# Four graph layers on one core: the steps between the probabilities and the value products of layers 1 and 3, in another order

## The reference, cut to what matters

```python
h = jnp.maximum(_layernorm(x), 0.0); x = x + _L0_gnn_ref(h, adj, adj, ...)   # attention, 8 heads of 32
h = jnp.maximum(_layernorm(x), 0.0); x = x + _L1_gnn_ref(h, adj, ...)        # attention, 4 heads of 64
h = jnp.maximum(_layernorm(x), 0.0); x = x + _L2_gnn_ref(h, adj, ...)        # gated tanh graph layer
h = jnp.maximum(_layernorm(x), 0.0); x = x + _L3_gnn_ref(h, adj, ...)        # attention, 4 heads of 64
```

```python
sim = jnp.einsum('bhid,bhjd->bhij', q, k) * scale
sim = jnp.where(adjacency_mask[:, None, :, :], sim, neg)
attn = jax.nn.softmax(sim, axis=-1)
out = jnp.einsum('bhij,bhjd->bhid', attn, v)   # the value products
return out.transpose(...).reshape(...) @ Wo + bo   # the output projection
```

## Time and profile before

| what | value |
|---|---|
| median of 3 runs | 2009.05 us (2006.77 to 2009.29) |
| profiled execution | 2007.06 us, its span 2005.1 us |
| mean granted clock of PE | 0.967 |
| PE busy | 1840.9 us, 92% |
| DVE busy | 1380.0 us, 69% |
| ACT busy | 996.7 us, 50% |
| POOL busy | 153.3 us, 8% |

### The profile page before, as it was taken

One profiled execution on the slowest core, in us unless ns is written; L12 is line 12 of the kernel. 1 busy time (PEld: TensorE's weight loads), 2 busy tenths in 40 slices (PEclk: granted clock), 3 DMA queues, 4 the chain that ended last, 5 costly groups with the idle time before them and its releaser, 6 DMA issues.

```text
span 2005.1 us, 58180 instructions
## 1 busy us (share of the span) xinstructions
PE 1840.9 (92%) x23611; PEld 1636.5 (82%) x23611; DVE 1380.0 (69%) x3777; ACT 996.7 (50%) x3707; POOL 153.3 (8%) x265
## 2 busy tenths in 40 slices
PE   6999999899999999999999999999998999999997
PEld 5878888878888878888878887878887888888886
DVE  4576677676777676777676677676767676677674
ACT  4455455454455454455455455455455445455452
POOL 0000000000000000000000000000000000000000
PEclk8899999999999999999999999899999999999898
DMA  6000000000000000000000000000000000000000
GB/s 195 1 9 13 13 8 12 13 8 13 13 8 13 12 8 13 13 8 12 13 13 8 13 13 8 12 13 8 13 13 8 12 13 8 13 13 8 12 7 6
DMA packets 36564, 30.62 MB, mean 15 GB/s; under 512 B 11600, under 2 KB 36176, under 8 KB 36368
## 3 DMA queue, kind: packets, MB, share of 16 engines
q1 hardware_dynamic: 36368, 27.48, 4.6%
HBM read 19.08 MB, written 8.39 MB: 14 GB/s over the span
## 4 chain that ended last, share of the span: by engine, by line
PE 75%; DVE 16%; issue 4%; ACT 4%; DMA 0%; DVEq 0%; SPq 0%; POOL 0%; POOLq 0%
PE ps L477 68%; PE ps L589 3%; PE ps L663 3%; DVE small L1069 2%; ACT probs L893 2%; DVE f L1228 1%; DVE xn L1081 1%; DVE f L1226 1%; DVE small L1075 1%; DVE oT L968 1%; DVE x L1233 1%; DVE kT L1128 1%; DVE probs L1158 1%; DVE probs L1142 1%; PE ps L786 1%
## 5 line engine op out<-in xcount | busy, mean ns | idle before, releaser
L477 PE MATMUL ps<-hT,w_hi 128*128 128x256 f32 x2560 | 487.8, 284 | 3.1 <-DVE w_lo L968 1.6
L477 PE MATMUL ps<-w_hi,hT 128*128 128x256 f32 (+1 forms) x1536 | 424.6, 344 | 0.0
L477 PEld LDWEIGHTS ps<-hT,w_hi 128*128 128x128 f32 x2560 | 406.6, 190 | 6.9 <-DVE w_lo L968 2.0
L893 ACT ACTIVATE probs<-probs,small 128x64 f32<-128x64 f32 x1024 | 342.0, 337 | 92.3 <-DVE small L1148 90.7
L477 PE MATMUL ps<-hT,w_lo 128*128 128x256 f32 x1280 | 332.8, 282 | 0.0
L477 PEld LDWEIGHTS ps<-w_hi,hT 128*128 128x128 f32 x1536 | 268.3, 188 | 42.7 <-DVE wh L1200 11.5
L464 POOL TENSOR_TENSOR small<-small,consts 128x1 f32<-128x1 f32 x256 | 151.3, 591 | 1824.6 <-DVE small L1077 1824.6
L477 PE MATMUL ps<-w_hi,oT 128*128 128x256 f32 x768 | 204.7, 331 | 57.6 <-DVE oT L968 48.4
L477 PE MATMUL ps<-w_lo,hT 128*128 128x256 f32 (+1 forms) x768 | 250.0, 337 | 0.0
L477 PEld LDWEIGHTS ps<-hT,w_lo 128*128 128x128 f32 x1280 | 243.5, 190 | 0.0
L477 PEld LDWEIGHTS ps<-w_hi,oT 128*128 128x128 f32 x768 | 147.9, 212 | 76.2 <-DVE oT L968 65.2
(11 more groups left out here) (126 smaller groups left out, 3329.8 us busy)
## 6 DMA issues: line engine op xcount, KB each, us to landing
x_next<-x SPq DMA_DIRECT2D x32, 256.0 KB, 2.7
out<-x SPq DMA_DIRECT2D x32, 256.0 KB, 2.2
raw_lo<-mats SPq DMA_DIRECT2D x6, 1024.0 KB, 10.5
adj<-adjq SPq DMA_DIRECT2D x64, 16.0 KB, 2.2
raw_hi<-mats SPq DMA_DIRECT2D x1, 1024.0 KB, 11.6
adjT<-adjt SPq DMA_DIRECT2D x64, 8.0 KB, 2.3
raw_lo<-mats SPq DMA_DIRECT2D x1, 512.0 KB, 8.3
raw_consts<-board_consts SPq DMA_DIRECT2D x1, 451.5 KB, 3.1
```

The lines of the kernel that those rows point to most:

```text
L477: return nc.tensor.matmul(o, lhsT, rhs, start=start, stop=stop, skip_group_check=True)
L893: last = fn(p, p, ACT.Exp, bias=ROWMAX[s][:, row:row + 1], accum_out=ROWSUM[s][:, row:row + 1])
```

## The change

```diff
             softmax += [("soft", a, u) for u in us[half:]] + [("pt", a, 1), ("pv", a, 0), ("heads", a, 1), ("pv", a, 1)]
+            if a > 0:
+                first, second = (softmax.index(("heads", a, 0)), softmax.index(("pv", a, 0)))
+                softmax = softmax[:first] + softmax[first + 1:second] + [("heads", a, n) for n in range(2)]
+                softmax += [("pv", a, n) for n in range(2)]
             return (norm_steps(a) + [(k, a, i) for k in ("q", "k", "v") for i in range(2)]
```

## The result

The changed kernel takes 2024.82 us (median of 4 runs, 2022.29 to 2029.01); the kernel before, beside it, 2007.91 us (4 runs, 1999.57 to 2009.29). The ratio is 1.0099, with a 95% interval of 1.0063 to 1.0135. It is 0.6 to 1.35% slower. Forecast were slower, 2034 us, and a range of 2012 to 2047. The profiled execution took 2025.52 us.

The account below looks back on a forecast made before the run. VectorE's in-order queue, not ScalarE's copies, was taken to set slot 1's output projection, clock falls being a second cost. 2007.06 + 11.5 (queue) + 14 (clock) = 2032.6, with the median 2.0 higher: 2034 us, range 2012 to 2047.

Parts of the forecast that it names:

- +0.74 us in a first meeting: Slot 0 in layer 1, slot 1 in layer 3: VectorE's reordered queue delays slot 1's output projection, fifteen times, +11.1 us.
- full-clock sum +11.5 us: Whole kernel without clock effects: first meetings +11.1, second meetings +1.6, last attention -1.2 us.
- The part of 0.40 us: VectorE, first meeting: soft 1 ahead of out 0 waits for slot 1's last exponential, making out 1 +0.40 us late.
- point 1: First meeting: slot 0's pv 0 moves behind max and bias; PE's first wait grows from 1.27 to about 2.3 us.
- The added wait of +0.06 us: PE, first meeting: slot 0's second turn waits for its probabilities, so slot 1's scores start at 1040.29 instead of 1040.23.
- Second meeting +0.1 us: Slot 0 in layer 3, slot 1 in layer 1: about 0.2 us earlier against +0.34 for norm 0; sixteen times, +1.6.
- The last attention, -1.2 us: Nothing runs beside it, so ScalarE's round trip is on the path; 1.2 us comes off, once.
- Clock +14 us: More PE idle time in first meetings makes 7 more halves fall in granted clock, at 2.0 us each; bounds 0 and +33.
- Switches and earlier products: PE: six fewer array-mode switches per loop turn and products 0.5 us earlier, counted only inside the +0.06 us.
- order alone: Rival: the queue costs its 11.5 us and the clock falls no oftener, 2021 us; chance 0.22.
- Faster: Rival: the copy's round trip decides, products end 0.5 us earlier in 31 meetings, fewer switches, 1993 us; chance 0.10.
- no change: Rival: the clock falls about six times less, offsetting the queue's cost, 2009 us; chance 0.05.

Follow-up runs that it names:

- e8: Changed kernel with VectorE's merge list altered to bring back its whole old order; ScalarE keeps its swapped pair: 1993.43 us, ratio 0.9960 to the kernel before.
- e1: Only PE walks the new step list, ScalarE and VectorE keep the old one: 1993.32 us against 2005.03 for the kernel before, ratio 0.9931.
- e2: Only VectorE and ScalarE walk the new step list, PE keeps the old one: 2032.34 us against 2005.03 for the kernel before, ratio 1.0150.
- e3: Changed kernel with PE's waits in the meetings filled by products whose result is never used: 1986.12 us, ratio 0.9906 to the kernel before.
- e4: Kernel before with PE's waits filled by products whose result is never used: 1974.68 us, ratio 0.9840 to the kernel before unfilled.
- e10: Changed kernel with, in the first meeting, out 0 ahead of soft 1 and slot 0's pv 0 ahead of max 1 again: 2005.15 us, ratio 0.9998.
- e5: Changed kernel with pv 0 ahead of the other slot's first normalisation again on VectorE, in both meetings: 2007.74 us, ratio 1.0031 to the kernel before.
- e6: Changed kernel with out 0 ahead of soft 1 again on VectorE in the first meeting: 2024.42 us, ratio 1.0093 to the kernel before.
- e9: Changed kernel with slot 0's pv 0 ahead of slot 1's second max and the bias again in the first meeting: 2013.93 us, ratio 1.0038.
- the filled kernels: e3, e4 and e7, with PE's waits filled by products whose result is never used: 1986.12, 1974.68 and 1972.06 us.
- e7: PE on the new list, VectorE and ScalarE on the old, PE's waits filled with unused products: 1972.06 us against 2003.38 for the kernel before, ratio 0.9848.

## Why the prediction was right, and where it was off

- *The queue of VectorE, not ScalarE's copy, sets when slot 1's projection starts.* Shown: e8 and e1 bring the loss down to nothing with PE's order new; e2 has all of the loss with PE's order old.
- *+0.74 us in a first meeting, full-clock sum +11.5 us.* The first meeting measured +0.65 us, the undisturbed half +0.70, and with the clock held the whole change costs 10 to 14 us (e3 against e4). That the medians give 11.4 is in part luck.
- *Its parts.* The normalisation stands 0.32 us ahead of the other slot's pv, as forecast; of it 0.2 us arrive in an undisturbed first half (58.90 in e10 against 58.70 in e8) and 0.3 us in a second one (59.30 against 59.00 in e5). The part of 0.40 us had the right size and half of its cause: "PE's work of point 1 is done by then and hides behind it" was too simple. Undoing either cause alone gains nothing on the path (e6, e9), undoing both does (e10).
- *The added wait of +0.06 us* for the probabilities: from slot 0's first turn to the mask 2.55 us, before 2.50. Right, and small.
- *Second meeting +0.1 us.* Half of what it was: +0.19 us on PE, and with the clock held the mean half of this kind goes from 59.29 (e4) to 59.54 us (e3), +0.25; the first kind goes from 58.90 to 59.59. By the mean with the clock free, 60.11 to 60.69, it cost as much as the first meeting, which is the clock's doing. I had let its count of falls stand as it was; it rose from 9 of 15 to 13.
- *The last attention, -1.2 us.* It did not come. From the first turn to the projection it is 2017.12 - 2013.50 = 3.62 us, before 1998.56 - 1994.83 = 3.73. One round trip is saved, but the second turn now waits 0.89 us for its probabilities. By these rows the full-clock sum is 15 x 0.65 + 16 x 0.19 - 0.1 = 12.7 us, where the prediction had 11.5.
- *Clock +14 us.* This is the mis-sized term: 4 to 10 us by the filled kernels. I had the number of disturbed halves right, even low (17 to 27, forecast 24), and the price of one too high. I took 2.0 us from the halves before. The filled kernel shows 1801.5 - 1773.0 = 28.5 us for 17, or 1.7 each; my 34.5 us also held PE's standstills of the last section. After the change it is 1819.6 - 1786.9 = 32.7 us for 27, or 1.2 each. One way in which a slow stretch costs little is the half of 59.50 us, where PE's longer wait before slot 1's projection takes it up; how many of the 27 went that way was not counted. With 7 for 14 the forecast would have been 2027 us against 2024.8. Another 1.1 us of the miss is the kernel before, 2009.05 us when I forecast and 2007.91 beside the change.
- *Switches and earlier products worth nothing but the +0.06.* Right for the path: e7 against e4 is 2.6 us at most, not the 15 of the rival. Wrong through the clock: PE's order alone gave 11.7 us (e1), nearly the rival's 1993 us by another way. The change as made lost that to VectorE's queue, and e8 keeps 0.4% of it by five small moves in one merge list.
- The rival "order alone" (2021 us) ended closer than the forecast, 3.8 us off against 9.2: the truth lies between the two, with a clock term that is there but smaller than I took. "Faster" and "no change" did not happen.

## What to carry to other kernels

When a step list is shared by engines and merged by position, a move that is meant for one engine re-orders the others too: write out every engine's queue before and after, and follow the one that has no pause, since the gain and the loss may be on different engines. If two entries of an in-order queue are both late, undoing either alone shows nothing; test them together before calling one harmless. Where the clock answers to the order as well, the effects of single moves need not add up. And ask of every wait on PE what it does to the clock: the order of PE alone moved the time by 12 us with its undisturbed halves nearly the same.

## What the runs showed of the hardware that I had not expected

- Useless products in PE's waits at the meetings (22610 - 21962 = 648 of them in the thirty halves of e3) kept the granted clock at 1.00 and made the kernels 1.6% (before), 1.9% (changed) and 1.1% (e1) faster. e4 at 1974.68 and e7 at 1972.06 us are the fastest versions found, and both beat the kernels given.
- With the clock at 1.00, some halves still take 0.6 to 1.0 us longer than their kind, 59.8 to 60.3 instead of 59.3 in e3, in the last third of its run. PE stands still there for up to 1.3 us some 44 us into the half (44 to 47 in the kernel before), and waits for nothing that the profile's view of waits names. The DMA records point to a cause. The instructions come in packets of 16 KB on a queue of their own (q8 in the page; 187 of them and 3.06 MB in the kernel before), five or six in a half. In all nine standstills of e3 and all ten of this kind in the kernel before, PE goes on 1.2 to 1.5 us after such a packet has landed. That fits a PE that had run out of instructions. No run changed the size of the code to test it.
- The setup ahead of the first layer-2 sum took from 119.0 to 128.9 us from kernel to kernel, though what they change is hardly in it. That is why the thirty halves are compared beside the times.
